# Twelve heads of a long convolution switched from float32 to three rounded passes, their halves made in the attention stage, and an earlier load of the second batch

## The reference

```python
x = x + attention(layernorm(x))        # elu(q)+1, elu(k)+1, 16 heads, kv = kp^T v, then @ o_w
# the convolution, 32 heads of 8 rows, 512 long:
kv  = einsum('bhil,bhjl->bijhl', k_, v_)          # k_ = v_ = context: 36 different products of 64
y   = causal_convolution(kv, ssm_kernel) + kv * D
out = einsum('bijhl,bhil->bjhl', y, q_)           # q_ = layernorm(x)
x = x + out
x = x + moe(layernorm(x))              # router, top 4 of 16 experts, one shared expert
```

## Time and profile before

| | |
|---|---|
| median of 3 runs | 862.4 us (861.37 to 862.54) |
| the profiled execution: its own time, its span | 863.55 us, 861.8 us |
| busy: PE, DVE, POOL, ACT | 98%, 63%, 52%, 44% of the span |
| all DMA traffic | 114.21 MB, mean 133 GB/s |
| granted TensorE clock, mean | 0.994 of full |

### The profile page before, as it was taken

The page is one execution under the profiler, slowest core; times in us unless marked ns, Lnnn a source line. Parts: engine busy times, 40 slices in busy tenths (PEclk is TensorE's granted clock), DMA queues, the critical chain, the costliest instruction groups (busy, mean ns, idle before and its releaser), DMA issues.

```text
span 861.8 us, 14219 instructions
## 1 busy us (share of the span) xinstructions
PE 842.3 (98%) x4346; PEld 704.0 (82%) x4346; DVE 543.4 (63%) x849; ACT 377.3 (44%) x608; POOL 445.9 (52%) x439
## 2 busy tenths in 40 slices
PE   8999999999999999999999999999999999999995
PEld 7888888889877777778888778888888888888884
DVE  6767767775657777888769875544455544555431
ACT  5313322333133533442552255555655555655552
POOL 1233223331068899884622343666666666656644
PEclk9999999999999999999999999999999999999998
DMA  8711101100026543440210397989999888999866
GB/s 283 241 39 21 29 24 37 37 12 13 1 62 196 163 131 110 123 131 17 93 63 7 104 323 171 218 204 215 191 189 214 212 213 195 189 196 223 205 119 86
DMA packets 55109, 114.21 MB, mean 133 GB/s; under 512 B 10721, under 2 KB 14817, under 8 KB 54945
## 3 DMA queue, kind: packets, MB, share of 16 engines
q1 hardware_dynamic: 38048, 73.28, 27.6%
q0 software_dynamic: 17024, 40.48, 25.6%
HBM read 83.07 MB, written 30.67 MB: 132 GB/s over the span
## 4 chain that ended last, share of the span: by engine, by line
PE 90%; DVE 5%; issue 2%; POOL 1%; ACT 1%; POOLq 0%; DVEq 0%; ACTq 0%
PE PS L206 20%; PE PS L208 20%; PE PS L207 20%; PE PS L217 17%; PE PS L1645 4%; PE PS L704 2%; PE PS L695 2%; PE PS L633 1%; PE PS L638 1%; PE PS L1582 1%; PE PS L1572 1%; PE PS L1612 1%; PE PS L1581 1%; PE PS L1564 1%; DVE KV L491 0%
## 5 line engine op out<-in xcount | busy, mean ns | idle before, releaser
L206 PE MATMUL PS<-QY_rounded,wh 128*128 128x512 f32 (+1 forms) x376 | 153.8, 409 | 0.0
L208 PE MATMUL PS<-QY_rounded,wl 128*128 128x512 f32 (+1 forms) x376 | 146.4, 389 | 0.0
L1360 POOL DMA_INDIRECT out_y<-QY,idy x72 | 114.5, 1590 | 44.7 <-ACT QY L1454 33.5
L207 PE MATMUL PS<-QY_rounded,wh 128*128 128x512 f32 (+1 forms) x312 | 120.1, 385 | 0.0
L1916 DVE TENSOR_TENSOR hTl<-hh,hTh 128x512 fp32r<-128x512 f32 (+1 forms) x39 | 27.5, 705 | 107.6 <-ACT hTh L1435 107.6
L1337 POOL DMA_INDIRECT xg<-xs_d,idx x64 | 76.7, 1199 | 28.8 <-POOL idx L1333 13.7
L208 PEld LDWEIGHTS PS<-QY_rounded,wl 128*128 128x128 f32 x376 | 71.1, 189 | 15.1
L217 PE MATMUL PS<-qER,Tz 128*128 128x288 f32 x320 | 81.1, 407 | 0.6 <-DVE QY L1062 0.4
L217 PE MATMUL PS<-prod,Tz 128*128 128x288 f32 x320 | 80.5, 407 | 0.2 <-DVE term L1045 0.2
L206 PEld LDWEIGHTS PS<-QY_rounded,wh 128*128 128x128 f32 x376 | 71.3, 190 | 11.1
L1454 ACT ACTIVATE QY<-PS,WPOS 128x512 f32<-128x512 f32 x76 | 52.4, 690 | 55.1 <-PE PS L208 55.1
(11 more groups left out here) (238 smaller groups left out, 1868.8 us busy)
## 6 DMA issues: line engine op xcount, KB each, us to landing
ws<-in_gu_w SPq DMA_DIRECT2D x38, 512.0 KB, 5.6
ws<-in_dn_w SPq DMA_DIRECT2D x20, 512.0 KB, 6.9
C<-in_ctx SPq DMA_DIRECT2D x32, 256.0 KB, 2.6
Tz<-kpad_d SPq DMA_DIRECT2D x32, 256.0 KB, 3.3
xs_d<-xn SPq DMA_DIRECT2D x16, 256.0 KB, 2.0
out_y<-X SPq DMA_DIRECT2D x16, 256.0 KB, 5.7
X<-in_x SPq DMA_DIRECT2D x1, 3072.0 KB, 16.6
xn<-in_xT SPq DMA_DIRECT2D x6, 512.0 KB, 3.3
```

The costliest lines, as they stand in the source:

```text
L206: pe.matmul(out_, lh, rh, start=first, stop=False)
L207: pe.matmul(out_, lh, rl, start=False, stop=False)
L208: return pe.matmul(out_, ll, rh, start=False, stop=last)
L1360: nc.gpsimd.indirect_dma_start(out=out, out_offset=bass.IndirectOffsetOnAxis(ap=idy[:, t:t + 1], axis=0), in_=yo[:, t], in_offset=None, co ...
```

## The change

Twelve odd heads, 7, 9, ... 29, are no longer convolved in float32. Their products are made on POOL during the attention, two heads per step in steps 1 to 6. ACT rounds them (`high_ahead`), POOL subtracts (`low_ahead`), and SP stores both halves in DRAM. The Toeplitz kernel gets its two halves once, ahead of step 1. In the convolution SP loads four tiles for such a head (`load_halves`: two Toeplitz halves of 256 KB, two product halves of 576 KB) and PE does 30 passes in place of 10 float32 matmuls. The other 20 heads use `Tz` and `C2` in their own order (`WHOLE`). The broadcast mean and rstd now go to `Tz[0]`, so the first two Toeplitz loads stand after the attention's last `z_done`. In the front, x of batch 1 is loaded ahead of the v weights, its `ln_stats` stand ahead of step 0, and `k_phi(0)` stands ahead of `qp(0)`. The shared expert's low halves are made in six pieces, not three, and PE's and SP's loops over heads are written out.

```diff
+AHEAD = 2
+HALVES = [2 * m + 1 for m in range(3, 3 + AHEAD * (B - DIRECT))]
+WHOLE = [h for h in range(CH) if h not in HALVES]
...
             sp.dma_start(qb[:], q_b).then_inc(qb_in, 16)
+            load_x(1, 2, 1)
...
-            load_x(1, 2, 1)
...
             with pool.Fori(DIRECT - 1, B - 1) as b:
                 rstd(pool, 0, b + 1, mv[0][:, :, 1])
+                s = b - (DIRECT - 1)
+                products_ahead(0, s)
+                low_ahead(0, s)
                 wait_apart(pool, xt_mr_in, 32 * b)
...
+                products_ahead(1, s)
                 rstd(pool, 1, b - 1)
+                low_ahead(1, s)
+            wait_apart(pool, lo_out, 16 * len(HALVES))
+            products(pool, 0)
             pool.wait_ge(qp_done, B)
...
+            def products_ahead(j, s):
+                pool.wait_ge(c2_in[j], s * 16 + 16)
+                wait_apart(pool, lo_out, s * (16 * AHEAD) + 16 * j)
...
+                for half in range(2):
...
+                    nc.gpsimd.tensor_tensor(o[:, :, 2 * half * CD:2 * (half + 1) * CD].rearrange("p a (s j) -> p a s j", s=2),
...
+            def low_ahead(j, s):
+                wait_apart(pool, ahead_hi, s * AHEAD + j + 1)
+                nc.gpsimd.tensor_tensor(ahead_prod.bitcast(F32R), ahead_prod, ahead_high, ALU.subtract).then_inc(ahead, 1)
...
+            def high_ahead(b, j):
...
+                act.activation(ahead_high.bitcast(F32R), ahead_prod, ACT.Copy).then_inc(ahead_hi, 1)
...
                 q_evac(b, first)
...
+                if made_ahead:
+                    high_ahead(b, 0)
                 k_evac(b)
...
                         qy_evac(b - 2)
+                    high_ahead(b, 1)
...
+                k_phi(b)
                     qp(b)
-                    ln_stats(0, b + 1)
...
+            ln_stats(0, 1)
             dve.wait_ge(memsets, 3)
             step(0, first=True)
...
+                def load_halves(n):
+                    k = n % 2
+                    for j, (t, dst) in enumerate(((TzHi[k], odd_h[k]), (TzLo[k], odd_l[k]))):
+                        src = bass.AP(tensor=kpad_hl_d.tensor, offset=(j * CH + HALVES[n]) * (KPAD + 1), ap=[[1, P], [1, D]])
+                        sp.dma_start(t[:], src).then_inc(halves_in[k], 16)
+                        sp.dma_start(dst[:].rearrange("p c b n -> p (c b n)"), prod_hl_d[j, n]).then_inc(halves_in[k], 16)
...
+                next_heads(0)
+                load_halves(0)
                 next_heads(1)
+                load_halves(1)
...
+                def convolve_halves(h, behind=None):
...
+                    pe.wait_ge(halves_in[k], 64 * (n // 2 + 1))
+                    pe.wait_ge(y_read[1], 2 * m)
+                    for c in range(DC):
...
+                        for r in range(c + 1):
...
+                            mm = three_pass(pe, o, TzHi[k][:, w].bitcast(F32R), TzLo[k][:, w].bitcast(F32R), odd_h[k][:, r].bitcast(F32R), odd_l[k][:, r].bitcast(F32R), r == 0, r == c)
```

More of the change, by code:

```diff
@@ L136, in decoder_program @@
         kpad_done, kpad_out = sem("kpad_done"), sem("kpad_out")
+        kpad_hl = [a[:].rearrange("p c s -> p (c s)")[0:CH, 0:KPAD + 1] for a in (aTh, aTl)]
+        ahead, ahead_hi = sem("ahead"), sem("ahead_hi")
+        hi_out, lo_out = sem("ahead_hi_out"), sem("ahead_lo_out")
+        halves_in = [sem(f"halves_in{k}") for k in range(2)]
+        NPROD = B * NPAIR
+        ahead_high = QY[:].rearrange("p c b s -> p c (b s)")[:, :, (B - 2) * S:(B - 2) * S + NPROD]
+        ahead_prod = prod[0][:].rearrange("p c b n -> p c (b n)")
+        AHEAD_MADE, AHEAD_LOW, AHEAD_STEP = (3, 7), (4, 8), 8
         tz_in = [sem(f"toeplitz_in{k}") for k in range(2)]
@@ L328, in _ @@
             pool.wait_ge(xns[1], TPB * B)
-            products(pool, 1, 0)
+            products(pool, 2)
         @block_.scalar
@@ L380, in qy_evac @@
                                    ACT.Copy).then_inc(qy_done, 1)
+            def high_ahead(b, j):
+                n = b - (DIRECT - 1)
+                wait_apart(act, ahead, n * AHEAD_STEP + AHEAD_MADE[j])
+                wait_apart(act, hi_out, n * (16 * AHEAD) + 16 * j)
+                act.activation(ahead_high.bitcast(F32R), ahead_prod, ACT.Copy).then_inc(ahead_hi, 1)
             def step(b, first=False, last=False):
+                made_ahead = not (isinstance(b, int) and b < DIRECT - 1) and not last
                 q_evac(b, first)
@@ L548, in step @@
                     a_lo(b - 1)
-                k_phi(b)
+                if not first:
+                    k_phi(b)
                 v_bias(b)
@@ L749, in _ @@
             step(B - 1, last=True)
-            convolve(pe, 0, 1, (3,))
+            convolve(pe, 1, (3,))
             att_t(B - 1, bank=4)
@@ L753, in _ @@
             transpose_tiles(xn[1], 0, trs[1])
-            convolve(pe, 0, 0, (2, 3))
+            convolve(pe, 0, (2, 3))
             oproj(B - 1, bank=4)
             pe.wait_ge(qy_done, TPB * (B - 1))
-            convolve(pe, 0, 0, (0, 1))
+            convolve(pe, 0, (0, 1))
             for t in range(TPB):
                 pe.wait_ge(x1_done, TPB * (B - 1) + t + 1)
-                warm((5, 3)[t], bank=4 + t)
+                for _ in range((5, 3)[t]):
+                    pe.matmul(PS[:, 4 + t], WH[:, 3, 0, 0:P], WH[:, 3, 0], start=True, stop=True)
                 pe.wait_ge(xns[1], TPB * (B - 1) + t + 1)
@@ L928, in _ @@
                     sp.dma_start(out[rows], zrow[:, 0:D]).then_inc(zero_out, 16)
-                with sp.Fori(3 + SLOT_T, normal_head(0) // 2) as i:
+                for i in range(3 + SLOT_T, normal_head(0) // 2):
                     next_heads(i)
@@ L933, in _ @@
                     store_rows(sp, e)
-                next_heads(CH // 2 - 2, last=True)
+                next_heads(CH // 2 - 2)
             @block_.gpsimd
@@ L961, in shared_lo @@
                                             ).then_inc(fixed_lo, 1)
-                with pool.Fori(2, 6) as i:
+                for i in range(2, 6):
                     pair_of_heads(i)
@@ L966, in _ @@
                 nc.gpsimd.tensor_tensor(gw_hl[:, :, 1], gw[:], gw_hl[:, :, 0].bitcast(F32), ALU.subtract).then_inc(fixed_lo, 1)
-                for part in range(NG - 1):
-                    pair_of_heads(6 + part)
-                    shared_lo(2 * part, 2 * part + 2)
+                for i in range(6, stream_head(0) // 2):
+                    pair_of_heads(i)
+                    shared_lo(i - 6, i - 5)
                 for i in range(stream_head(0) // 2, CH // 2):
-                    products(pool, i, 1)
                     for e in range(EARLY):
@@ L1094, in normal_across @@
                     return mm
-                with pe.Fori(1, stream_head(0) // 2) as i:
-                    for k in range(2):
-                        convolve(pe, i, k)
-                for h in range(stream_head(0), CH):
+                def convolve_halves(h, behind=None):
+                    n, m = HALVES.index(h), h // 2
+                    k = n % 2
+                    pe.wait_ge(halves_in[k], 64 * (n // 2 + 1))
+                    pe.wait_ge(y_read[1], 2 * m)
+                    for c in range(DC):
+                        o = PS[:, DC + c].rearrange("p (b n) -> p b n", n=YGAP)[:, :, 0:NPAIR]
+                        for r in range(c + 1):
+                            w = slice((c - r) * P, (c - r + 1) * P)
+                            mm = three_pass(pe, o, TzHi[k][:, w].bitcast(F32R), TzLo[k][:, w].bitcast(F32R), odd_h[k][:, r].bitcast(F32R), odd_l[k][:, r].bitcast(F32R), r == 0, r == c)
+                        if behind is not None and c == DC - 1:
+                            mm = behind()
+                        mm.then_inc(conv_ps[1], 1)
+                for h in range(2, CH):
                     behind = None
```

194 lines of the change are left out of this document (127 added, 67 removed).

## The result

The changed kernel takes 872.37 us in the median of four runs (868.67 to 874.54) against 862.37 us before: a ratio of 1.0108, interval 1.0087 to 1.0128, 1.1% slower. The profiled execution took 872.45 us with a span of 869.7 us; before it was 863.55 us with 861.8 us.

A forecast was written before the change was run, and what follows sets the result against it. PE was taken to bound attention and convolution. Terms -10.2 + 3.0 + 11 - 0.75 = +3.05 on the profiled 863.55 gave 866.6, as a median 865.4 us; own range 860 to 871, 8 in 10 range 854 to 872.

The forecast's parts named there:

- The passes: Convolution: rounded passes of 288 columns take 0.1335 us, a head 4.00 us, 0.85 less than now; twelve heads give -10.2 us.
- The loads: Start of the convolution: head 6's Toeplitz load queues behind 3.31 MB, so PE waits 1.5 to 4 us once; +3.0 us.
- The attention: Attention steps: POOL's 2.63 us subtractions hold DVE operations, 2.0 us lost a step; +11 us, bounds 0 and 16.
- (1): Steady attention step: the second `ln_norm` waits 2.45 us for POOL's subtraction, so the k projection starts 1.0 us later.
- (2): Steady attention step: the second `x_bias` waits for POOL's subtraction, `a_lo` ends at 136.2, and `oproj` loses 0.2 us.
- (3): Steady attention step: work on `xz` takes turns with `k_phi`, `x_add` ends at 144.2, and `t2` loses 0.8 us.
- Step 1: First attention step with added work: loses only about 0.5 us, since its `xz` work stands later.
- The products alone cost nothing: Attention on POOL: the products, in pieces of 1.05 us, use up no spare time and cost nothing.
- The front: Ahead of `kv(0)`: half of PE's 1.49 us wait goes, as `ln_stats(0, 1)` no longer stands between; -0.75 us (0 to -1.5).
- at worst 0.3 us for each of four pairs: Convolution heads with extra transposes (18 to 27): DVE comes close to PE; expected cost nothing, at worst 0.3 us a pair.
- The rival that the attention keeps its pace: Attention: the three spare times cover the added POOL work, so steps lose nothing; 854.5 us, chance 0.26.

The follow-up runs named there:

- e3: Changed kernel with the loads of `gw` and the shared weights issued after `next_heads(2)`, behind head 6's Toeplitz load; 868.12 us.
- e1: Changed kernel with each POOL subtraction of 1152 elements cut into four of 288; 869.72 us.
- e2: Changed kernel with each POOL subtraction reduced to one element per chunk, all other work and transfers kept; 864.32 us.
- e6: e5 with DVE's rounding remainder `x3_low` placed ahead of that head's products instead of behind them; 861.87 us.
- e12: e6 with the transposed x (`xz`) loaded earlier and each step's first low half again one whole subtraction, the second in four pieces; 860.03 us.
- e5: Changed kernel with subtractions cut into four of 288 and the gate's and scorer's weights loaded behind the pieces of head 2; 863.12 us.
- e7: Changed kernel with each step's first low half formed on POOL behind the work on the transposed x, not ahead of it; 883.63 us.

## Why the prediction was right, and where it was not

The forecast was 865.4 us, 0.35% slower; measured is 872.37, 1.1% slower. The direction is the one foreseen, and most of the costs came from where the forecast put them. The size is off by 7 us: beyond the forecast's own 860 to 871, and at the very end of the range of 8 in 10 (as a time 0.4 us past its 872, as a ratio 1.0108 for 1.0111). By its steps:

- **The passes** (-10.2): right. 0.133 us as interpolated, 8.83 us a pair for 8.85; twelve heads give 12 x 0.87 = -10.4 us.
- **The loads** (+3.0): the mechanism right, the size not. The wait was 4.24 us, just over the 4 of the bound, and the DMA engines were at their full share until it ended; what I had left out is the clock, 0.58 of full speed in the 4 us after it, another 1.55 us. The sum should have had +5.8. e3 shows that it is the loads of `gw` and `ws`: behind head 6's they cost nothing.
- **The attention** (+11): +11.3 measured, from partly other pieces. The prediction's own pieces add up to 11.5, not 11: six times (1), five times (2) and (3), and 0.5. (1) `ln_norm` held: 2.35 us, as reckoned at 2.45, though the first of the pair and not the second; the k projection lost 0.64 to 0.73 instead of 1.0, and five times, not six: the last time, at 212.28, `ln_norm` is held for 3.35 us too, and PE does not wait. That is 3.3 us for 6.0. e1 shows that it is the length of the subtraction. (2) `x_bias` held, 0.2 a step: wrong, it was ahead of the subtraction, nothing for 1.0. (3) `t2`, 0.8: it was 1.0 to 1.5, 6.1 us for 4.0. The prediction had the statistics arrive 0.3 us behind the subtraction and turns with `k_phi` stretch the work on `xz` to 6.1 us; in the trace POOL is idle for them 0.85 to 1.47 us, and the work takes 5.3 us (139.78 to 145.05). Step 1, reckoned at 0.5, lost 2.5 (a part of it is the first wait of (1)): there the statistics are written 0.9 us later on SP's queue, behind a power operation of POOL that took 1.78 us instead of 0.71 beside DVE's `qp`, and `z_lo` takes 2.50 us instead of 1.90. That the total fits within 0.3 is thus partly luck. "The products alone cost nothing" is right for a steady step (e2).
- **The front** (-0.75): -1.0. `kv(0)` starts at 27.96 instead of 29.05, and PE's wait ahead of it falls from 1.49 to 0.83 us, near the half taken.
- **Left out**: 1.8 us in three places of the late heads ("at worst 0.3 us for each of four pairs"), which e6 brings back in part, and the time outside the span, 2.75 us in the profiled execution (2.2 to 2.3 in the other three) against 1.75 before. The sum of the measured terms is -1.0 + 11.3 - 10.4 + 5.8 + 1.8 = +7.5 of the span's 7.9; what is missing lies in the convolution, and I can't place it. Why the time outside the span grew is open.

Against its own execution the sum was 5.85 us too low (866.6 to 872.45): 2.8 in the loads, 1.8 in the late heads, 1.0 outside the span, the rest in small terms. The other 1.1 us lie in the step from the execution to the median: 1.15 us for the kernel before, 0.08 for the changed one.

The rival that the attention keeps its pace was worth 854.5 us. Runs e2 and e12 show how near these variants come to it: 864.3 without the subtraction but with the wait at head 6, 860.0 with it in the lengths of e12 and the loads moved.

Open is the rest of the attention's loss in e12, 209.87 against 204.73 us: 3.1 us of waits ahead of `t2`, and in step 1 1.3 ahead of `oproj` and 1.1 ahead of `att` (1.0 before). A second product buffer, which would free POOL from the stores, was not tried.

## What to carry to other kernels

When POOL gets work with SBUF inputs beside DVE, ask how long one instruction is and which DVE instruction stands behind it: in steps 2 to 6 the same work cost 8.7 us whole, 5.2 in pieces (e1) and 3.3 with the length chosen by the spare time of whoever is held (e12, which also loads `xz` earlier). Short pieces protect an urgent DVE operation, and lengthen POOL's own chain when POOL is the one that is late.

Before moving an operation, follow its store: what waits for the buffer, and which small transfer now stands behind the large one. Three moves that looked free cost 11 to 16 us (the low half later), 2 more (rstd first) and 16.5 more (`xz` loaded earlier on top), by a store of 576 KB, one in-order ACT, and the low clock behind each wait of PE that grew.

A long wait of PE can cost more than its length: look at the granted clock of the next stretch before you look for a second cause. And where two traces differ by 1.5 to 2 us, look first for a stretch of low clock that only one of them has.

## What the runs showed of the hardware

- One `tensor_scalar` of 512 elements on DVE, alone 0.54 us, sat out a POOL subtraction of 2.68 us and took 2.89 (3.35 us for the pair); with the subtraction in pieces of 288 the pair takes 1.97. The hold works both ways: POOL's 2-element `tensor_scalar` took 1.18 instead of 0.22 us beside DVE's `qp`, its power operation 1.78 instead of 0.71.
- After 4.24 us without a pass, the granted clock was 0.58 of full speed over the next 4 us and full again after that; head 6 took 6.40 us instead of 4.85. After 2.30 us (e12) it was the same 6.40. A wait of 2.45 us in the changed kernel's attention had no low clock behind it, one of 2.49 in e5 had: 0.66 over 60 to 65 us.
- A write of 2 KB issued right behind 1.1 MB on the same queue took 6.85 us until the next issue (e7), 4.09 us when the same 1.1 MB were issued 6 us ahead of it, 3.26 us when little stood ahead of it.
